# Local attention stack on one core: pieces of a unit in another order on all engines, token columns by transfers, a two-input clamp

## The reference

```
x = x + 0.5 * stack(layernorm(x))
x = x + latent_attention(layernorm(x))
x = x + 0.5 * stack(layernorm(x))

stack, for each of 6 layers:
    x = attn(shift(x)) + x          # shift: the upper 64 columns come from the token before
    x = ffn(shift(x)) + x
attn: q, k, v = x @ Wqkv            # 16 heads of 64
      q, k = l2norm(q)*qs, l2norm(k)*ks; both rotated, q and k scaled by position
      windows of 32 tokens, each looks at itself and the window before: softmax(q k^T * 8 + mask) v, then @ Wo
ffn:  layernorm, @ W1 (128 -> 2*341), a * gelu(gate), @ W2
```

## Time and profile before

| | us |
|---|---|
| median of 3 runs | 5789.85 |
| the three runs | 5765.26, 5789.85, 5873.94 |
| the profiled execution | 5868.65 |
| its span, first to last instruction | 5866.9 |
| PE busy (share of the span) | 5284.4 (90%) |
| DVE busy | 4178.8 (71%) |
| ACT busy | 3627.3 (62%) |
| POOL busy | 3415.1 (58%) |
| mean granted TensorE clock, share of full | 0.916 |

### The profile page before, as it was taken

One profiled execution on the slowest core, in us unless ns is written; L12 is line 12 of the kernel. 1 busy time (PEld: TensorE's weight loads), 2 busy tenths in 40 slices (PEclk: granted clock), 3 DMA queues, 4 the chain that ended last, 5 costly groups with the idle time before them and its releaser, 6 DMA issues. The chain is left out here.

```text
span 5866.9 us, 143623 instructions
## 1 busy us (share of the span) xinstructions
PE 5284.4 (90%) x46548; PEld 3143.6 (54%) x46548; DVE 4178.8 (71%) x8715; ACT 3627.3 (62%) x10714; POOL 3415.1 (58%) x3696
## 2 busy tenths in 40 slices
PE   7999999999999985799999999799999999999997
PEld 4656656665665652233434433466566656566564
DVE  6888888888888872343434343788888888888885
ACT  4777777777777760022222222677777777777785
POOL 6877777777777761000001000777777777777774
PEclk8999999999999995587979787899999999999998
DMA  2121121211112111000000000212111121111111
GB/s 66 39 53 41 42 52 37 54 41 50 45 36 53 42 31 21 0 1 1 1 1 1 1 1 1 67 37 53 41 49 45 37 53 42 49 44 39 51 41 30
DMA packets 266274, 203.85 MB, mean 35 GB/s; under 512 B 76284, under 2 KB 263192, under 8 KB 264728
## 3 DMA queue, kind: packets, MB, share of 16 engines
q1 hardware_dynamic: 265496, 194.08, 13.0%
HBM read 41.87 MB, written 1.05 MB: 7 GB/s over the span
## 5 line engine op out<-in xcount | busy, mean ns | idle before, releaser
L528 POOL TENSOR_TENSOR rot<-t 128x512 f32<-128x512 f32 x768 | 972.9, 1267 | 860.6 <-DVE t L816 418.4
L523 POOL TENSOR_TENSOR inv<-ssm,neg_half 128x8 f32<-128x8 f32 x768 | 1325.3, 1726 | 0.0
L710 ACT ACTIVATE prob<-ps,nmx,inv 128x96 f32<-128x96 f32 x3072 | 1278.6, 425 | 0.6
L593 PE MATMUL ps<-w_qkv,xs 128*128 128x512 f32 x1536 | 877.5, 654 | 63.1 <-issue 30.9
L1267 ACT ACTIVATE ptl<-ps_l 128x1024 f32<-128x1024 f32 (+1 forms) x288 | 281.4, 977 | 968.0 <-PE ps_l L1142 735.7
L697 ACT COPY vt<-ps 128x256 f32<-128x256 f32 x768 | 286.4, 373 | 785.5 <-PE ps L629 785.5
L660 PEld LDWEIGHTS ps<-pt,vs 96*64 96x64 f32 x12288 | 427.2, 139 | 388.4 <-issue 351.6
L629 PE MATMUL ps<-w_qkv,xs 128*128 128x256 f32 x1536 | 549.7, 440 | 89.3 <-ACT ots L678 87.1
L825 DVE TENSOR_SCALAR ssm<-ss 128x8 f32<-128x8 f32 x768 | 595.6, 775 | 26.4
L710 ACT ACTIVATION_READ_ACCUMULATOR prob<-ps,nmx,inv 128x1 f32 x3072 | 608.2, 198 | 0.0
L816 DVE TENSOR_TENSOR t<-ps,tab_s 128x256 f32<-128x256 f32 x1536 | 575.1, 416 | 0.0
(11 more groups left out here) (203 smaller groups left out, 8891.5 us busy)
## 6 DMA issues: line engine op xcount, KB each, us to landing
vs<-vt SPq DMA_DIRECT2D x768, 96.0 KB, 2.2
vs<-vt SPq DMA_DIRECT2D x768, 64.0 KB, 2.1
vs<-vt SPq DMA_DIRECT2D x768, 32.0 KB, 1.8
w_qkv<-in_L_ffn_Wqkv SPq DMA_DIRECT2D x48, 384.0 KB, 3.5
w_o<-in_L_ffn_Wo SPq DMA_DIRECT2D x12, 512.0 KB, 4.0
w<-in_L_ffn_W SPq DMA_DIRECT2D x12, 341.0 KB
wcos<-const_wc SPq DMA_DIRECT2D x2, 1024.0 KB, 4.9
wsin<-const_ws SPq DMA_DIRECT2D x2, 1024.0 KB, 7.3
```

What stands on the lines that cost most here:

```text
L523: nc.gpsimd.tensor_tensor(inv[:, n % 4], ssm[:, n % 2], neg_half[:, 0:2 * HU], ALU.pow).then_inc(z["inv_ready"], 1)
L528: nc.gpsimd.tensor_tensor(rot[:, n % 4], t1[:, n % 2], t2[:, n % 2], ALU.add).then_inc(z["rotated"], 1)
L593: pe.matmul(ps[:, j % 2, :], xs[:, j // UT % 2, :], w_qkv[:, 0:2, u * 256:(u + 1) * 256], start=True, stop=True).then_inc(z["qk_ready"], 1)
L710: e = nc.scalar.activation(prob[:, n % 2, h, :], scores[:, h % 2, h // 2, :], ACT.Exp, scale=inv[:, n % 4, h:h + 1], bias=nmx[:, n % 2, h: ...
```

## The change

The order of the pieces in a slot changes on every engine, and so do lags: V goes from lag 1 to 2, S from 3 to 4, and PT, O and y each one slot later.

- PE: QK, y, S, V, PT, then the feed-forward piece, then RT, then O (before: RT ahead of the feed-forward piece).
- ACT: sq, the feed-forward pieces (Gelu among them), the copy of V, exp, the copy of RT, the copy of O, the copy of PT. Before: copy of O, feed-forward pieces, sq, copy of V, copy of PT, exp, copy of RT, Gelu. The copy of O now follows in the slot of its O instead of the next.
- DVE: t1, t2, rec, prob, mx, y's addition, nmx, ss, clamp, feed-forward piece. Before: rec, prob, t1, mx, y's addition, nmx, t2, ss, clamp, the copies to `xs`, feed-forward piece.
- POOL: rot, inv, knorm, carry, tables. Before: tables, carry, inv, rot, knorm.
- `xs` is written by two transfers on SP's queue, issued three slots or more before the tile is used, with a semaphore for each of the two buffers.
- The clamp is a scalar_tensor_tensor with `ss` as both tensors in place of a tensor_scalar.
- The transfer of query, key and value weights is split: query and key first, value later. The small vectors of the feed-forward part are loaded ahead of its matrices.
- The feed-forward phases stay where they were, named by a table PHASE; the tail after the last layer has one lag and three empty slots more.

```diff
-LAG_R, LAG_V, LAG_T, LAG_S, LAG_P, LAG_O, LAG_Y = 1, 1, 2, 3, 4, 5, 7
+LAG_R, LAG_V, LAG_T, LAG_S, LAG_P, LAG_O, LAG_Y = 1, 2, 2, 4, 5, 6, 8
+PHASE = dict(shift=0, mean=1, centre=1, square=2, var=2, eps=2, rstd=3, diag=3, spread=4, scale=4,
+             gate=(5, 6, 7), gate_copy=(6, 7, 8), gelu=8, up=(9, 10, 11), prod=(9, 10, 11), down=12, add=12)
...
+            def tokens(tile):
+                cols = tile % TILES * P
+                sp.dma_start(xs[0:64, tile % 2, :], x_a[0:64, cols + 1:cols + 1 + P]).then_inc(z[f"xs_in_{tile % 2}"], 16)
+                sp.dma_start(xs[64:P, tile % 2, :], x_a[64:P, cols:cols + P]).then_inc(z[f"xs_in_{tile % 2}"], 16)
...
+                    tile = j // UT + 2
+                    if j % UT == UT - 1 and not (part == "last" and tile >= TILES):
+                        if tile == TILES:
+                            sp.wait_ge(z["x_a_ready"], (L + L0) * G + 2)
+                        elif tile % 4 == 0 and part != "first":
+                            sp.wait_ge(z["x_a_ready"], (L + L0) * G + (tile // 4 - G + 2))
+                        tokens(tile)
...
@@ PE, in slot @@
+                if p is not None:
+                    feed_forward(L, p, g)
                 if live(LAG_T):
                     pe.wait_ge(z["k_normed"], done(LAG_T))
...
-                if p is not None:
-                    feed_forward(L, p, g)
                 if live(LAG_O):
...
@@ DVE, in slot @@
-                    nc.vector.tensor_scalar(ssm[:, j % 2], ss[:, j % 2], 1e-24, None, ALU.max).then_inc(z["clamped"], 1)
-                if live(0) and j % UT == 1:
...
-                    shifted(tile % TILES, tile % 2)
+                    nc.vector.scalar_tensor_tensor(ssm[:, j % 2], ss[:, j % 2], 1e-24, ss[:, j % 2], ALU.max, ALU.max).then_inc(z["clamped"], 1)
```

More of the change, by code:

```diff
@@ L395, in strips_in, with tokens_in @@
             return ((L + L0) * (UNITS // UT) + ((j - lag) // UT + 1)) * 48
+        def tokens_in(L, tile):
+            return (L + L0) * (TILES // 2 * 32) + (tile // 2 + 1) * 32
         def feed(j, part):
             g, p = divmod(j - LAG_Y, 16)
-            return (p, g - 1) if p <= 12 and not (part == "first" and g < 1) else (None, None)
+            return (p, g - 1) if not (part == "first" and g < 1) else (None, None)
         def group_no(L, g):
@@ L413, in walk @@
                     slot(L, j, "steady")
-            for j in range(UNITS, UNITS + LAG_Y + 13):
+            for j in range(UNITS, UNITS + LAG_Y + 16):
                 slot(DEPTH - 1, j, "last")
@@ L512, in slot @@
                     scaled_tables((j // UT + 1) % TILES, (j // UT + 1) % 2)
[L513 to L532, removed]
             pool.wait_ge(z["sc_in"], (L0 + k + 1) * SC)
@@ L674, in slot @@
                 p, g = feed(j, part)
-                if live(LAG_O + 1):
-                    n = (j - LAG_O - 1) % 8
-                    act.wait_ge(z["o_ready"], done(LAG_O + 1))
-                    nc.scalar.copy(ots[:, n].rearrange("p a t -> p (a t)"), ps[:, 6, HV]).then_inc(z["ot_read"], 1)
-                if p == 2:
-                    act.wait_ge(z["ln_centred"], norm_no(L, g) + 1)
-                    nc.scalar.activation(f_sq[:, :], f_xc[:, :], ACT.Square).then_inc(z["ln_squared"], 1)
-                if p is not None and 6 <= p <= 8:
-                    m = p - 6
-                    w = CH[m][1]
-                    act.wait_ge(z["gate_up"], group_no(L, g) * 3 + m + 1)
-                    nc.scalar.activation(f_gate[0:w, m, :], ff[0:w], ACT.Identity, bias=vec[0:w, 6 + m:7 + m]).then_inc(z["gate_read"], 1)
                 if live(0):
@@ L691, in slot @@
                     nc.scalar.activation(sq[:, j % 2], ps[:, j % 2, :], ACT.Square).then_inc(z["squared"], 1)
+                if p == PHASE["shift"]:
+                    act.wait_ge(z["x_b_ready"], group_no(L, g) * 4 + 4)
+                    nc.scalar.copy(f_src[0:64, :], x_b[0:64, 1 + g % G * GT:1 + (g % G + 1) * GT]).then_inc(z["sh_lo"], 1)
+                if p == PHASE["square"]:
+                    act.wait_ge(z["ln_centred"], norm_no(L, g) + 1)
+                    nc.scalar.activation(f_sq[:, :], f_xc[:, :], ACT.Square).then_inc(z["ln_squared"], 1)
+                if p in PHASE["gate_copy"]:
+                    m = PHASE["gate_copy"].index(p)
+                    w = CH[m][1]
+                    act.wait_ge(z["gate_up"], group_no(L, g) * 3 + m + 1)
+                    nc.scalar.activation(f_gate[0:w, m, :], ff[0:w], ACT.Identity, bias=vec[0:w, 6 + m:7 + m]).then_inc(z["gate_read"], 1)
+                if p == PHASE["gelu"]:
+                    act.wait_ge(z["gate_read"], group_no(L, g) * 3 + 3)
+                    nc.scalar.activation(f_gate[:, :, :], f_gate[:, :, :], ACT.Gelu).then_inc(z["gelu_ready"], 1)
                 if live(LAG_V):
```

152 lines of the change are left out of this document (85 added, 67 removed).

## The result

| | before | after |
|---|---|---|
| median of the runs side by side, us | 5790.01 (4 runs) | 5953.74 (4 runs, 5930.18 to 6028.41) |
| ratio | | 1.023 [1.017, 1.030] |
| profiled execution, us | 5868.65 | 5938.63 |
| first to last QK, both stacks together, us | 4201 | 4322 |

A forecast was written before the change was run, and what follows sets the result against it. PE was taken to stand still 8.7 us in sixteen slots, waiting mostly for RT's copy and around Gelu. DVE's longer round offsets the gain: 5868.65 + 3 + 8 = 5880 us profiled, scaled 5800, no change; range 5560 to 5920.

The forecast's parts named there:

- The deciding step: On DVE and POOL: rot starts 0.05 us ahead of prob, which waits for all of rot; 1.07 us more DVE a slot.
- rival C: On PE: the mask's stalls go over to V, waiting for O's copy; 5800 us, chance 0.50 together with the forecast.
- whenever POOL stands waiting for t2: On POOL: the condition under which rot is ahead of prob by 0.05 us and prob waits for the whole rot.
- Rival A: rot does not hold prob: sixteen slots 82.2 us, 5550 us scaled, 5670 if half escape; chance whole or half 0.32.
- Rival B: The clamp on DVE meets knorm and waits some 0.6 us in eight turns: 6030 us scaled, half 5915; chance 0.18.
- the price of the clamp: On DVE: the clamp, placed beside inv, costs between 0.08 and 0.7 us; 0.10 was taken.
- t1, t2, ss and mx don't stretch: On DVE: these instructions keep their length beside POOL's; mx and nmx together were counted at 0.65 us.
- DVE starts mx 0.55 ahead of PT: In turns out of slots with y: DVE's 4.5 us round less 0.55 plus y's 0.20 makes 4.15 at p = 15.
- sixteen slots at 87.5: One feed-forward group, PT to PT: turns of 87.3 us plus 0.2 for clamps that meet knorm, against 87.44 before.
- One more slot of lag in each stack, some 4 us, makes +8: The added slot of lag in each stack costs some 4 us, +8 us in the profiled execution.
- 48 groups (12 layers of 4): The difference of one sixteen-slot group, 87.5 against 87.44 us, counted for 48 groups: +3 us.
- Hidden terms: Token transfers covered by three slots; weight split and small vectors 0, bounds -2 and +4 us a layer; ACT's end-of-slot copies 0.

The follow-up runs named there:

- kernel 1: The changed kernel, but POOL waits for prob of the same slot before it starts rot: ratio 0.986 of before, stack time 4112 us.
- kernel 6: The changed kernel with lag 7 for y in place of 8, which puts Gelu back into slot 63: ratio 1.035 of before, stack time 4362 us.
- kernel 7: The changed kernel with rot waiting for prob, Gelu at the end of ACT's slot and lag 7 for y: ratio 0.999 of before.
- kernel 5: The changed kernel with the two xs token copies back on DVE in place of the transfers: ratio 1.060 of before, stack time 4488 us.
- kernel 10: The changed kernel with rot waiting for prob and the two xs copies back on DVE: ratio 1.007 of before, stack time 4222 us.
- kernel 4: The changed kernel with Gelu moved to the end of ACT's slot, behind the copy of PT: ratio 1.009 of before, stack time 4233 us.
- kernel 9: The changed kernel with rot waiting for prob and Gelu at the end of ACT's slot, lag 8 for y kept: ratio 0.975 of before.

## Why the prediction was wrong

I forecast no change, 5800 us with a range of 5560 to 5920; it is slower by 2.3%, 5954 us. The mechanism was right, and the sum built on it was not.

- **The deciding step was right, in the loop.** rot starts 0.04 us ahead of prob (0.05 forecast) and keeps it out for its whole length, in the median 1.64 us (1.65). PE waits at PT for prob, the mask's stalls are gone (45.5 to 4.8 us), and V did not inherit them (rival C). That it holds "whenever POOL stands waiting for t2" failed in the first layers, where rot starts behind prob.
- **Rival A's price.** Sixteen slots without the hold, 82.2 us by A, measured 83.5 and 85.1 in the first layer of after (granted clock 0.98 and 0.96). With the wait of kernel 1 they are 86.0 in the mean and 85.0 at the full clock, since nmx is held instead.
- **Rival B did not happen.** The clamp is at 167 ns; inv, ahead of it on POOL, does not hold it. I had the price of the clamp right.
- **Failed: "t1, t2, ss and mx don't stretch", with nmx left at its 0.65 beside mx.** nmx reads two inputs in SBUF, as prob does. I gave such a hold to prob and the clamp only. Where POOL is late by the tables and rot misses prob, it catches nmx; exp is late, and y with it: 0.39 us at p = 14.
- **Mis-sized: "DVE starts mx 0.55 ahead of PT".** It measured 0.39 and 0.40, and the round was closed without the 0.13 from prob to PT: 0.29 us in each turn out of a slot with y that DVE bounds, at p = 3, 11 and 15. At p = 11 I had also no wait for the up product.
- **Mis-sized: sixteen slots at 87.5.** At the full clock they take 89.0, +1.5; the four named turns are 1.7 of it, and the rest nearly cancels.
- **Failed: the clock was no term of the sum.** I compared a group of before at its full clock with a sum at the full clock, and took the dips to be the same. They are not: the 24 ordinary groups (with no return in them or just ahead) have 91.95 us in the mean against 88.31, +3.6, and not +1.5. The other 2.1 stand in the Gelu turn and the next, and go with the lower level of the clock.
- **Failed: "One more slot of lag in each stack, some 4 us, makes +8".** The tails, from the last QK to the last sum into x_a, grew by 8.7 and 7.9 us, twice what I allowed for both; why, no run shows. And the lag also moves each phase of the feed-forward part against the return of the loop. The return cost 2.2 us beside a Gelu before and costs 5.1 alone now, 2.8 us at each of eight returns. Kernels 6 and 7 were meant to test it: 7 does show the overlap, but a lag of 7 can't collect it in this order.
- **Failed: "48 groups (12 layers of 4)" alike.** The first layers are 20 us shorter each than before, 40 in all, which the sum did not have. That is luck: without it the miss would be larger by as much.
- **The account.** The groups give 40 x 3.6 = 146 us. Over the returns 18 more are measured (each return adds 3.5 us to two groups after and 1.3 before; the dips make it less than the 23 by the turns), and the first layers take off 40: 124, of the 120 measured in the stacks. The tails, 17 us, lie outside them.
- **Hidden terms.** The token transfers cost nothing, as forecast, and freed more than their 0.9 us in four slots: kernels 5 and 10 put them at 3.6% and 2.1%. The weight split and the small vectors weren't tried alone.
- **The range.** The measured time stands 34 us above its upper end. The range had the clamp's uncertainty in it and none for the dips and the returns.

## What to carry to other kernels

When two engines hold each other out by who starts first, a wait on the producing side is a cheap control: one wait before POOL's long instruction turned 1.023 into 0.986. Look for the places where such a tie already falls the other way, here the layer outside the loop: they show the price of the hold without a new kernel. List every two-input instruction of DVE, whatever its size, that may start inside each long one of POOL; freeing one only passes the hold to the next, and pays until another engine is late. And when a lag changes, look where each long piece lands against the return of the loop: it may have been hidden there at no cost.

## What the runs showed of the hardware that I had not expected

- The hold does not depend on the size of DVE's instruction: with 4 elements a partition nmx took up to 1.22 us instead of 0.16 while rot ran, and the clamp with 8 elements 0.74 us instead of 0.17, in either form.
- A copy with a single input, 64x128 in float32, is held too: 0.6 us beside knorm, 0.22 beside inv (kernel 5).
- The converse fails for inv: POOL's power on 8 elements runs for 1.65 to 1.96 us, and the clamp beside it still takes 167 ns.
- At a loop's return all engines stand for 3 to 4 us (DVE 3.06, PE 3.82), but the Gelu of before with its table load of 1.28 us, which stands ahead of the return in ACT's order, runs while PE stands.
- A stall of PE of 2.41 and 1.13 us within one slot was followed by a granted clock of 0.65 over the next 4 us, and the Gelu turn and the next one were longer by 1.46 and 1.10 us than in the group before, where the stalls were 1.71 and 1.33 us and the PT rows show no slower pace. I can't say from these rows which stall brings the dip. With Gelu at the end of ACT's slot (kernel 4) 20 of 32 groups had none, against 2 of 32, and in kernel 9 it was 11 against the 2 of kernel 1: the place of one long instruction on ACT decided how often PE's clock fell.
